# Gated attention and FFN on one core: the forget-gate product and two growth levels moved, the sum over heads split between ScalarE and GpSimd

## What is computed

```
q, k, v, w = short_conv(h @ W*, c*)              # 4 taps per channel, then SiLU; w is l2-normalised per head
g    = log_sigmoid(h @ Wf1 @ Wf2)                # the forget gate, per head and slot
beta = sigmoid(h @ Wb)
step: Sk = Sk * exp(g) + k (beta w)';  Sv = Sv * exp(g) + (beta w) v'
      o_t = softmax(q . Sk * SCALE) . Sv
o = o * rsqrt(mean(o*o) + EPS) * norm_w * sigmoid(h @ Wg1 @ Wg2 + bg2)
x = layernorm(x + o @ Wo)                        # a sum over the 16 heads
```

## Time and profile before

| | before |
|---|---|
| runs | 2284.19 us median of 3 (2282.63 to 2293.97) |
| profiled execution | 2293.06 us, its span 2291.3 us |
| busy, share of the span | PE 88%, DVE 80%, ACT 57%, POOL 55% |
| chain that ended last, by engine | PE 40%; DVE 38%; issue 14%; POOL 5%; ACT 2% |
| TensorE's granted clock | mean 0.961 |
| acc, L546 | four 128x256 additions a slot on DVE |

### The profile page before, as it was taken

One profiled execution on the slowest core, in us unless ns is written; L12 is line 12 of the kernel. 1 busy time (PEld: TensorE's weight loads), 2 busy tenths in 40 slices (PEclk: granted clock), 3 DMA queues, 4 the chain that ended last, 5 costly groups with the idle time before them and its releaser, 6 DMA issues.

```text
span 2291.3 us, 41351 instructions
## 1 busy us (share of the span) xinstructions
PE 2013.9 (88%) x12192; PEld 1647.6 (72%) x12192; DVE 1842.2 (80%) x4347; ACT 1304.6 (57%) x3679; POOL 1269.4 (55%) x2205
## 2 busy tenths in 40 slices
PE   7789899898888998899889998999989989997576
PEld 6577777777777777777777777777777777776465
DVE  1788888888888888888888888888888988885555
ACT  2565566666665656556565665656666656563322
POOL 4455655566555665556555665556665556654233
PEclk8899999999999999999999999999999999998788
DMA  3000000000000000000000000000000000000000
GB/s 67 1 3 14 2 1 15 1 13 3 14 2 14 2 1 15 1 14 3 14 2 14 2 14 2 1 15 1 13 3 14 2 14 2 1 5 1 17 18 18
DMA packets 41732, 20.65 MB, mean 9 GB/s; under 512 B 13744, under 2 KB 41520, under 8 KB 41520
## 3 DMA queue, kind: packets, MB, share of 16 engines
q1 hardware_dynamic: 41520, 18.10, 2.9%
HBM read 15.99 MB, written 2.10 MB: 8 GB/s over the span
## 4 chain that ended last, share of the span: by engine, by line
PE 40%; DVE 38%; issue 14%; POOL 5%; ACT 2%; DVEq 1%; DMA 1%; SPq 0%; POOLq 0%; ACTq 0%
DVE conv L477 12%; PE proj_ps L600 9%; PE mix_ps L687 8%; DVE wT L470 8%; DVE U L459 6%; PE V_ps L655 5%; PE tr_ps L624 4%; DVE acc L546 4%; PE V_ps L633 4%; PE work_ps L714 4%; PE proj_ps L1221 3%; POOL W L299 2%; ACT conv L332 2%; DVE V_ps L566 2%; POOL fused_lo L863 2%
## 5 line engine op out<-in xcount | busy, mean ns | idle before, releaser
L477 DVE SCALAR_TENSOR_TENSOR conv<-proj_ps,coefs,conv 128x511 f32<-128x511 f32 (+2 forms) x768 | 564.9, 736 | 70.6 <-ACT conv L332 61.4
L812 POOL TENSOR_TENSOR A_lev<-A,masks 128x256 f32<-128x256 f32 x448 | 331.1, 739 | 248.4 <-ACT A L375 248.4
L299 POOL TENSOR_TENSOR W<-W,tot 128x256 f32<-128x256 f32 x384 | 262.5, 684 | 166.1 <-PE mix_ps L687 165.3
L687 PE MATMUL mix_ps<-W,U 128*128 128x128 f32 x1792 | 308.9, 295 | 40.9 <-POOL W L299 34.5
L687 PEld LDWEIGHTS mix_ps<-W,U 128*128 128x128 f32 x1792 | 256.9, 195 | 90.2 <-issue 71.3
L655 PE MATMUL V_ps<-A_lev,UT 128*128 128x128 f32 x1792 | 284.3, 281 | 20.4 <-DVE V_ps L566 20.2
L655 PEld LDWEIGHTS V_ps<-A_lev,UT 128*128 128x128 f32 x1792 | 240.4, 191 | 49.5 <-DVE V_ps L566 46.1
L593 DVE COPY_PREDICATED A<-masks,mix_ps 128x256 f32<-128x256 uint32 x448 | 268.9, 600 | 6.7 <-PE mix_ps L687 6.6
L566 DVE TENSOR_TENSOR V_ps<-V_ps,tot 128x256 f32<-128x256 f32 x384 | 168.7, 439 | 107.2 <-PE V_ps L655 105.5
L470 DVE TENSOR_TENSOR wT<-wT,tot 128x128 f32<-128x128 f32 x768 | 215.7, 322 | 40.8 <-DVE U L459 0.9
L390 ACT ACTIVATE UT<-tr_ps 128x512 f32<-128x512 f32 (+1 forms) x256 | 139.6, 545 | 164.4 <-PE tr_ps L624 164.3
(11 more groups left out here) (174 smaller groups left out, 4810.3 us busy)
## 6 DMA issues: line engine op xcount, KB each, us to landing
acc<-in_L_attn_hidden_states SPq DMA_DIRECT2D x1, 2048.0 KB, 8.5
w_raw<-in_L_attn_Ww SPq DMA_DIRECT2D x16, 128.0 KB, 2.3
w_raw<-in_L_attn_Wq SPq DMA_DIRECT2D x16, 128.0 KB, 2.3
w_raw<-in_L_attn_Wk SPq DMA_DIRECT2D x16, 128.0 KB, 2.4
w_raw<-in_L_attn_Wv SPq DMA_DIRECT2D x16, 128.0 KB, 2.4
wo_raw<-in_L_attn_Wo SPq DMA_DIRECT2D x16, 128.0 KB, 2.2
out_x<-acc SPq DMA_DIRECT2D x4, 512.0 KB, 2.9
wf_head<-in_L_attn_Wf SPq DMA_DIRECT2D x16, 64.0 KB, 2.0
```

What stands on the lines that cost most here:

```text
L299: nc.gpsimd.tensor_tensor(w, w, block_tot(u3.par, lev, 0), ALU.mult).then_inc(W_step, 1)
L477: nc.vector.scalar_tensor_tensor(y_, proj_ps[:, CONV_BANK[i], 0:T - back], filt(u, i, KW - 1 - back), y_, ALU.mult, ALU.add).then_inc(conv ...
L687: last = nc.tensor.matmul(mix_ps[:, half, p * P:(p + 1) * P], Ulev(u3, lev)[:, p * P:(p + 1) * P], after_odd(W[:, p * T // 2:(p + 1) * T / ...
L812: nc.gpsimd.tensor_tensor(dst, diag_after_odd(lev), mask_cols(lev), ALU.mult)\
```

## The change

1. The addition of a head's output to acc is split. ScalarE copies work_ps times rms into a new tile `y_sb` (four of 128x256), where VectorE's additions stood (r = 6 and 7). GpSimd adds y_sb to acc one slot later (a unit `u5`), right behind the first growth of W. There are 68 slots then. TensorE waits for ScalarE's copies (`ys_done`) where it waited for the additions.
2. The forget-gate product goes from ahead of the last key-query product to behind the projection of q. Mix product 1 is put in its place. The tanh and the `gates` copy on ScalarE, and the three gate products on GpSimd, come later accordingly; on GpSimd the rms chain takes the gate products' old place.
3. On VectorE level 0 of `grow_U` comes before the first k tap and level 1 behind it; level 2 is done at the end of the same slot (`GROWN_EARLY = 3`).

```diff
-        PROJ_AT = (1, 3, 4, 5)
+        PROJ_AT = (1, 2, 4, 5)
-        GROWN_EARLY = 2
+        GROWN_EARLY = 3
+        def scale_output(act, u4, t):
...
+            nc.scalar.activation(y_sb[:, t, :], work_ps[:, t // 2, (t % 2) * HID:(t % 2 + 1) * HID], ACT.Copy,
+                                 scale=rms[:, u4.par % 2, t:t + 1]).then_inc(ys_done, 1)
+        def add_heads_output(pool, u5, t):
+
+            pool.wait_ge(ys_done, u5.count(4, t + 1))
+            wait(pool, acc_done, u5.count(4, -12 + t))
+            a = acc[:, u5.par * C + t, :]
+            nc.gpsimd.tensor_tensor(a, a, y_sb[:, t, :], ALU.add).then_inc(acc_done, 1)
...
@@ GpSimd
                     if u3:
                         grow_W(pool, u3, i)
+                    if s.u5 and i == 0:
+                        for t in range(C):
+                            add_heads_output(pool, s.u5, t)
-                    if u1 and i == 2:
-                        for lv in (1, 2, 3):
-                            gate_products(pool, u1, lv)
-                    if u4 and i == 4:
+                    if u4 and i == 2:
...
+                    if u1 and i == 4:
+                        for lv in (1, 2, 3):
+                            gate_products(pool, u1, lv)
@@ ScalarE
+                    if u4 and r in (6, 7):
+                        scale_output(act, u4, 2 * r - 12)
+                        scale_output(act, u4, 2 * r - 11)
@@ VectorE
-                    if u4 and r in (6, 7):
-                        add_heads_output(dve, u4, 2 * r - 12)
-                        add_heads_output(dve, u4, 2 * r - 11)
+                    if u1 and r in (5, 6):
+                        grow_U(dve, u1, r - 5)
                     if u1 and r == 8:
                         conv_tap(dve, u1, 2, 2)
-                        grow_U(dve, u1, 0)
...
                     if u1 and r == 8:
-                        grow_U(dve, u1, 1)
+                        grow_U(dve, u1, 2)
@@ TensorE
-                if u1:
-
-                    pe.wait_ge(head_f, 16 * (u1.h + 1))
-                    wait(pe, conv_step, u1.count(12, 0))
-                    nc.tensor.matmul(proj_ps[:, 1, :], wf2_head[:, :], f1T[:, u1.par * T:(u1.par + 1) * T], start=True,
-                                     stop=True).then_inc(proj_ps_ready, 1)
+                if u3:
+                    mix_products(pe, u3, 1)
```

More of the change, by code:

```diff
@@ L41, in unit @@
             return Unit(off - lag) if 0 <= off - lag < units else None
-        self.u1, self.u2, self.u3, self.u4 = (unit(lag) for lag in range(4))
+        self.u1, self.u2, self.u3, self.u4, self.u5 = (unit(lag) for lag in range(5))
         self.edge = not 3 < off < units
@@ L49, in slots @@
 def slots(heads, seqs):
-    for n in range(heads * seqs + 3):
+    for n in range(heads * seqs + 4):
         yield Slot(n, heads * seqs)
@@ L159, in build @@
         tg = sb("tg", [P, T])
+        y_sb = sb("y_sb", [P, C, HID])
         def setup_weights(buf):
@@ L536, in values @@
                                      scale=fac[:, u2.par, c:c + 1]).then_inc(vN_done, 1)
-        def add_heads_output(dve, u4, t):
+        def scale_output(act, u4, t):
             if t == 0:
-                dve.wait_ge(rms_step, u4.count(4, 4))
-                wait(dve, acc_done, u4.count(4, 0))
+                act.wait_ge(rms_step, u4.count(4, 4))
+                wait(act, acc_done, u4.count(4, 0))
             if t % 2 == 0:
[L544 to L547, removed]
+                act.wait_ge(y_ps_ready, u4.count(2, t // 2 + 1))
+            nc.scalar.activation(y_sb[:, t, :], work_ps[:, t // 2, (t % 2) * HID:(t % 2 + 1) * HID], ACT.Copy,
[5 more added lines that the diff above has]
+            nc.gpsimd.tensor_tensor(a, a, y_sb[:, t, :], ALU.add).then_inc(acc_done, 1)
         def descend(dve, u2, r):
@@ L813, in _ @@
                             .then_inc(Alev_done, 1)
-                    if u1 and i == 2:
-                        for lv in (1, 2, 3):
-                            gate_products(pool, u1, lv)
-                    if u4 and i == 4:
+                    if u4 and i == 2:
                         r = rms[:, u4.par % 2, :]
                         z = Z[:, u4.par, :]
-                        wait(pool, acc_done, u4.count(4, -4))
+                        wait(pool, ys_done, u4.count(4, -4))
                         pool.wait_ge(a_done, u4.count(4, 4))
@@ L921, in _ @@
                 if u1:
-                    act.wait_ge(proj_ps_ready, u1.count(5, 2))
-                    wait(act, gate_set, u1.count(1, 0))
-                    nc.scalar.activation(fexp[:, :], proj_ps[:, 1, :], ACT.Tanh, scale=0.5).then_inc(fexp_done, 1)
                     tanh(act, u1, 0)
@@ L928, in _ @@
                         evac_UT(act, u2, (2, 2, 3, 3, 4, 5)[r])
-                    if u1 and r == 0:
-                        gates(act, u1)
                     if u4 and r == 0:
@@ L938, in _ @@
                         tap(act, u1, 1)
+                        act.wait_ge(proj_ps_ready, u1.count(5, 3))
+                        wait(act, gate_set, u1.count(1, 0))
+                        nc.scalar.activation(fexp[:, :], proj_ps[:, 1, :], ACT.Tanh, scale=0.5).then_inc(fexp_done, 1)
                     if u2 and r == 2:
                         values(act, u2)
+                    if u1 and r == 2:
+                        gates(act, u1)
                     if u1 and r == 3:
@@ L1252, in _ @@
                         project(u1, 2)
-                    if u3 and r + 1 < IN_CHUNK:
+                    if u3 and 0 < r < IN_CHUNK - 1:
                         mix_products(pe, u3, r + 1)
@@ L1259, in _ @@
                         project(u1, 1)
+                        pe.wait_ge(head_f, 16 * (u1.h + 1))
+                        wait(pe, conv_step, u1.count(12, 0))
+                        nc.tensor.matmul(proj_ps[:, 1, :], wf2_head[:, :], f1T[:, u1.par * T:(u1.par + 1) * T], start=True,
+                                         stop=True).then_inc(proj_ps_ready, 1)
                     if u4 and r in (5, 6):
@@ L1292, in _ @@
                     if u4:
-                        pe.wait_ge(acc_done, u4.count(4, 4))
+                        pe.wait_ge(ys_done, u4.count(4, 4))
                     else:
```

10 lines of the change are left out of this document (5 added, 5 removed).

## The result

The changed kernel takes 2209.7 us, the median of 4 runs (2209.12 to 2210.29); the kernel before takes 2286.96 on the same chips. The forecast was 2213, faster.

A forecast was written before the change was run, and what follows sets the result against it. TensorE and VectorE were taken to bound the kernel in turns, neither full. Clean slots 0.5 x 63 = 32 us, excess 42, end -2: 72 us off the 2284.19 median, 2212, given as 2213; range 2183 to 2262.

The forecast's parts named there:

- Stretch 1, VectorE: VectorE behind mx: level 2 leaves, so w taps end 0.93 us earlier and TensorE's first-level product starts 1.55 us earlier.
- Additions: GpSimd behind W's first growth: four additions at 0.65 us each, taking back 0.1 to 0.3 of 1.87 us; 1.6 kept.
- Forget-gate product put back: TensorE behind the second projection: the product costs 1.10 us on the path, leaving 0.5 of 1.6 us a slot.
- Stretch 3: VectorE from the third projection to the next mx: additions leave, levels 0 to 2 enter; net -0.25 to +0.1 us, taken as 0.
- ScalarE: Four scaled copies, 1.6 to 2.7 us, fit in the 3.82 us idle before the Sv copy and cost nothing.
- The excess: Slots longer than the clean one, 55 us in all, from U_top meeting W's growth and TensorE clock falls: 42 us go.
- The end: One slot more, with four additions and a copy behind the last product: 2 us added.
- Rival B: Chance 0.20: the order works but TensorE's clock falls as often; only some 14 us of excess go, giving 2240 us.
- Rival C: Chance 0.09: level 1's products wait out GpSimd's 1.01 us power, V_ps step 1.4 us late; slower, 2322 us.
- Rivals D and E: D (0.07): additions 0.80 or more, no change, 2283 us. E (0.09): additions 0.62, all excess gone, 0.75 a slot, 2184 us.

## Why the prediction was right, point by point

- *Stretch 1, VectorE.* Right. The w taps were to end 0.93 earlier and the first-level product to start 1.55 earlier; they came 0.78 and 1.50 earlier, counted from mx. The difference is the first level behind mx, whose copy now takes 0.79 instead of 0.65 beside qk. TensorE's idle piece ahead of the first-level product is 0.59; 0.85 was expected.
- *Additions.* Right in place, a little short in size: 0.70 each, not 0.65 (2.79 for four). TensorE's wait for W was to take back 0.1 to 0.3 us, though the prediction's own times, 1001.45 and 1001.8, make it 0.35; mix product 2 came at 11.18, 1.42 earlier instead of 1.6.
- *Forget-gate product put back.* The price of 1.10 was too high: that is the length of the row, which runs on after the next instruction has started. From start to start the product takes 0.86 (0.93 in the old place). But the step is the one that failed in substance: the prediction credited the 1.87 us to the change as a whole and asked only what it cost to put the product back. It did not ask what the growth levels alone would bring. The run without the move shows 0.65 of the 1.42 to come from it, against 0.86 paid. The move was a loss of 16 us inside a gain of 77.
- *Stretch 3.* Right. Taken as 0 with -0.25 to +0.1; the V_ps step came 0.18 later behind the k tap, TensorE's wait went from 0.29 to 0.47, and mx now waits for TensorE. It comes 0.04 behind the transposes (983.70) instead of 0.19. With that the clean slot's gain adds up: 1.42 - 0.86 - 0.18 + 0.15 = 0.53.
- *ScalarE.* Right. A scaled copy takes 0.47, four lie in the wait before Sv, which still has 1.01 us left of 3.82.
- *The excess.* Right in kind, too small in size: 55 of 55 us went, not 42. The growth levels alone take all of it. The run with the forget-gate product alone separates two of its sources: there the meetings of U_top and the growth of W stay and the clock does not fall. So breaking up the 1.82 us was enough, as the prediction had it, and so was shortening it to 0.98. The third source, GpSimd's splitting of the weights beside levels 0 and 1 in every fourth slot, was overlooked; the run without the growth levels shows it to be the largest part of what they are worth inside the change. That it went too is luck: the levels were moved for another reason.
- *The end.* Too small: +2 was taken, the ramp and the tail cost 6.7. The ramp is long in the runs with the moved product (100 to 102 us before the first mx) and 97 to 98 in those without it, but for 100.7 with the sum alone. Its cause stays open.
- *Rival B* (the clock still falls) fell: 1.00. *Rival C* (level 1 waits for the power) fell by this row and the one of level 1's products above. They start at 977.97, the second of the two just behind the power's start, and both are done at 978.50, 0.67 before the power ends:

```profile
978.16 1.01 POOL L849 TENSOR_TENSOR fac<-fac,consts 128x4 f32<-128x4 f32 x1
```

- *Rivals D and E*: the additions cost 0.70 and not 0.80, and E's full excess came true, but not its 0.75 a slot.

The forecast came nearer than its sum. The sum was worked out in the profiled execution, where it said 72 and the two spans differ by 83: the clean slot was 0.54 for 0.5, the excess 55 for 42, ramp and tail 6.7 for 2. It was then taken from the median of the runs, which lay 8.9 below that execution. The changed kernel's four runs lie within 1.2 us and have no such long execution, and between the medians 77 were saved. So 2213 against 2209.7 is partly luck.

On the rule that was weighed (the Trainium skill, "SBUF — State Buffer", "Who interferes with whom": the one that holds the shared ports holds them for its whole instruction): the additions ahead of W bear it out for 128x256 operations. A pair of VectorE products takes 0.9 us longer beside additions of 0.75 each, and taps that read PSUM are not held up: three w taps take 2.24 beside the additions, and took 2.24 before. The 2.31 of the v taps, which the prediction put down to the growth of W, is not a cost of that work either: with the additions ahead of W the growth has ended at 1017.38 when they start at 1017.96, and they take 2.31 all the same. For the power on 128x4, 1.01 us long, a lock for the whole instruction is not what the trace shows, and the measurement decides; level 1's pair took 0.53 beside it instead of 0.49.

## What to carry to other kernels

Where two engines hand over in turn, read one undisturbed slot and ask of each part of a change what it gives when the others are there: parts that gain alone need not gain together, and one of them can be a loss inside a gain. Work sent to GpSimd is hidden only where VectorE does not use its kind of access at the same time; four additions cost 132 us more in one place than in another. And if slots differ in length, the excess over the clean slot is a term of its own; here it was more than the change in the clean slot. List all slots and sort the long ones by what is in them: one slot read as clean and one as disturbed showed two of three causes.

## What the runs showed of the hardware that I had not expected

- Behind an idle gap of TensorE of 1.82 us the granted clock went to 1.2 GHz in 25 of 89 slots, counted over the kernel before and the sum over heads alone: in 16 of 28 where a gap of 0.59 stood before it, in 9 of 61 without. With gaps of 0.59, 0.90 and 0.59 it fell in none of 29 slots (forget-gate product alone); with 1.27 and then 0.90 (additions ahead of W) in 19 of 60, in 8 of them already at the end of the 1.27.
- A 1.01 us power on 4 elements per partition on GpSimd lengthened a pair of VectorE products beside it by 0.04 us (0.49 to 0.53), while additions on 256 elements, 0.75 us each, lengthened such a pair by 0.9 (0.49 to 1.39).
